# Four GNN layers on one core: the first layer's turns, gathers and normalizations in another order, the fourth layer's source rows made in the third, and loads issued a chunk sooner

## The reference

```python
x = _layernorm(x + attention(x, edge_attr))              # "layer 0"
x = _layernorm(x + relu(([x, mean of x[src]] @ W1 + b1) @ W2 + b2))   # "layer 1"
x = _layernorm(x + segment_sum((x @ weight)[src, rel], dst))          # "layer 2", 8 relations
x = _layernorm(x + update_by_node_type([relu(x), 3 typed message sums]))  # "layer 3"
```

## Time and profile before

| what | value |
|---|---|
| median of 3 runs | 1717.78 us (1715.58 to 1718.99) |
| profiled execution | 1722.77 us, span 1721.0 us |
| mean granted TensorE clock | 0.923 |
| busy: PE, DVE, ACT, POOL | 1390.8, 1410.1, 1120.2, 1230.3 us |
| layer 0 with its gathers | to 657 us |
| layer 1 | 667 to 957 us |
| layer 2 | 1009 to 1328 us |
| layer 3 | from 1343 us |

### The profile page before, as it was taken

How to read it: one execution, slowest core, us unless ns; L and a number is a source line. 1 busy time by engine, 2 the same in 40 slices (tenths; PEclk the granted TensorE clock), 3 DMA queues, 4 the chain that set the end, 5 groups by cost and what they waited for, 6 DMA issues and landing times.

```text
span 1721.0 us, 22842 instructions
## 1 busy us (share of the span) xinstructions
PE 1390.8 (81%) x6078; PEld 902.0 (52%) x6078; DVE 1410.1 (82%) x3005; ACT 1120.2 (65%) x2769; POOL 1230.3 (71%) x910
## 2 busy tenths in 40 slices
PE   4687777777777755787878589999998699999995
PEld 2454444544445434666666355555555355555552
DVE  4688888888888874998889679999998578877774
ACT  1567877778777783999999836666665344334442
POOL 7877777777788877778888387776330668888874
PEclk9678999999999987989999889999999899999998
DMA  7334444444434343677777535555543434333320
GB/s 169 85 68 101 112 98 98 105 104 112 99 98 108 82 130 73 187 201 192 197 196 194 161 87 144 150 141 137 148 119 94 99 94 101 99 94 93 98 74 22
DMA packets 165796, 205.06 MB, mean 119 GB/s; under 512 B 66825, under 2 KB 97920, under 8 KB 165668
## 3 DMA queue, kind: packets, MB, share of 16 engines
q1 hardware_dynamic: 108068, 179.45, 38.8%
q0 software_dynamic: 57600, 24.15, 8.0%
HBM read 147.12 MB, written 70.80 MB: 127 GB/s over the span
## 4 chain that ended last, share of the span: by engine, by line
PE 48%; DVE 16%; ACT 12%; issue 12%; POOL 9%; DMA 2%; SPq 1%; POOLq 0%; DVEq 0%; ACTq 0%
PE po L1323 22%; PE pt L1312 6%; POOL slot_all L528 6%; DVE masked L937 5%; DVE bst L732 4%; ACT x L1039 3%; PE pb L1329 2%; PE pb L1561 2%; PE po L1318 2%; PE po L1383 2%; PE pc L1431 2%; ACT so L1039 2%; PE pc L1312 2%; ACT do L1039 2%; ACT res L1039 1%
## 5 line engine op out<-in xcount | busy, mean ns | idle before, releaser
L528 POOL DMA_INDIRECT xs<-target_rows,slot_all x236 | 316.9, 1343 | 160.9 <-issue 68.8
L1039 ACT ACTIVATE x<-y,nmr,rst 125x128 f32<-125x128 f32 x800 | 322.3, 480 | 43.2 <-DVE nmr L757 43.2
L1323 PE MATMUL po<-wnt,rt 128*125 128x384 f32 x800 | 290.1, 508 | 0.0
L1312 PE MATMUL pt<-ident,x 125*128 125x125 f32 x800 | 134.6, 295 | 111.2 <-issue 82.3
L1323 PEld LDWEIGHTS po<-wnt,rt 128*125 128x125 f32 x800 | 158.3, 201 | 92.3 <-issue 14.4
L1323 PE MATMUL po<-wnt,run 128*125 128x384 f32 x600 | 201.5, 486 | 0.0
L535 POOL DMA_INDIRECT out_rows<-do,last_all x100 | 146.6, 1466 | 60.7 <-issue 40.0
L528 POOL DMA_INDIRECT xs<-in_x,src_all x100 | 133.8, 1338 | 53.7 <-issue 53.7
L1312 PEld LDWEIGHTS pt<-ident,x 125*128 125x128 f32 x800 | 100.1, 154 | 136.9 <-issue 100.9
L1039 ACT ACTIVATE do<-yd,nmr,rst 125x128 f32<-125x128 f32 x400 | 163.5, 482 | 6.2 <-DVE nmr L757 6.2
L1039 ACT ACTIVATE res<-sel,nmr,rst 125x128 f32<-125x128 f32 x400 | 163.5, 482 | 3.8 <-DVE nmr L757 2.6
(11 more groups left out here) (186 smaller groups left out, 3024.5 us busy)
## 6 DMA issues: line engine op xcount, KB each, us to landing
xin<-in_x SPq DMA_DIRECT2D x100, 224.0 KB
out_rows<-res SPq DMA_DIRECT2D x100, 224.0 KB
same<-same_d SPq DMA_DIRECT2D x75, 250.0 KB, 4.1
source_rows<-so SPq DMA_DIRECT2D x75, 224.0 KB
target_rows<-do SPq DMA_DIRECT2D x75, 224.0 KB
xs<-source_rows SPq DMA_DIRECT2D x59, 224.0 KB
rel<-in_etype SPq DMA_DIRECT2D x50, 250.0 KB, 4.8
xd<-target_rows SPq DMA_DIRECT2D x46, 224.0 KB
```

What stands on the lines that cost most here:

```text
L528: return nc.gpsimd.indirect_dma_start(out=to, out_offset=None, in_=table, in_offset=bass.IndirectOffsetOnAxis(ap=index, axis=0), bounds_ch ...
L1039: last = A(to[:, j, :], y[:, j, :], ACT.Identity, scale=rst[s][:, k:k + 1], bias=nmr[s][:, k:k + 1])
L1312: last = nc.tensor.transpose(tile_of(to, j), rows_[:, j, :], ident[0:R, 0:R])
L1323: last = mm(po[0:R, j * 512:j * 512 + NT * D], left(j), wnt[:, k, :, :].rearrange("k t d -> k (t d)"), start=start, stop=stop, skip_group_ ...
```

## The change

**In layer 0** the gathers of a chunk are split: the four of the sources wait only for what reads xs, then five marks instead of six, then the four of the targets. PE turns the sources of chunk c+2 ahead of the products of dense chunk 2c, and ACT takes its normalizations and evacuations in another order. SOONER goes from 19 to 13, so 52 instead of 76 slot gathers stand ahead of layer 1; the other 48 are issued within layer 1.

**In layers 1 and 2** the second normalization `so3` leaves layer 1. DVE makes instead one factor per row (factors1, two small operations per chunk, into again_all), and in layer 2 ACT makes the same rows as xs times that factor (source_rows2, four activations per chunk). SP stores them in layer 2.

**On SP** the first loads of layers 1, 2 and 3 stand ahead of the last stores of the layer before; the sums of layer 3 go to other buffers (aux and rel3).

The core of the diff:

```diff
-        MARKS = 6
+        MARKS = 5
         MARKED = -(-T * EC // MARKS)
-        SOONER = 19
...
+        SOONER = 13
+
...
                 sp.wait_ge(q["nS"], c + 1)
                 for part in PARTS:
                     sp.dma_start(rows(s_rows[1])[c][part, :], flat(so[b])[part, :]).then_inc(q["stS"][b], 16)
-                for part in PARTS:
-                    sp.dma_start(rows(s_rows[2])[c][part, :], flat(so3[b])[part, :]).then_inc(q["stS"][b], 16)
...
-            store_sources0(EC - 1)
...
+            rows1(2)
+            targets1(1)
+            store_sources0(EC - 1)
             store_targets0(EC - 2)
-            rows1(2)
             store_targets0(EC - 1)
-            targets1(1)
...
             def sources2(c):
                 k, q, o = c % 3, ph[2], ph[1]
                 sp.wait_ge(q["tS"], at(c - 2))
-                sp.wait_ge(o["stS"][c % 2], counted(c, 2 * ROWS))
+                sp.wait_ge(q["nS"], at(c - 2))
+                sp.wait_ge(o["stS"][c % 2], counted(c, ROWS))
...
+            def store_sources2(c):
+                b, q = c % 2, ph[2]
+                sp.wait_ge(q["nS"], c + 1)
+                for part in PARTS:
+                    sp.dma_start(rows(s_rows[2])[c][part, :], flat(so3[b])[part, :]).then_inc(q["stS"][b], 16)
...
+            for c in range(EC):
...
+                if c == EC - 1:
+                    sources2(0)
+                    relations2(0)
+                    sources2(1)
+                    relations2(1)
+                    sums2(0)
+                    targets2(0)
+                    sums2(1)
+                    sources2(2)
+                if c >= 1:
+                    store_sources1(c - 1)
+                    store_targets1(c - 1)
+                    store_dense(d - 7)
             store_targets1(EC - 1)
...
             stored(1)
+            store_sources2(0)
             sources2(3)
+            store_sources2(1)
...
+                sp.wait_ge(q["vA"], at((c - 1) * NT))
+                if c < 2:
+                    sp.wait_ge(ph[1]["vA"], EC)
+                sp.dma_start(aux[b][:, :], to_all(same_d, c)).then_inc(q["sm"][b], 16)
+                sp.dma_start(rel3[b][:, :], to_all(etype3, c)).then_inc(q["sm"][b], 16)
+
...
+                if c == EC - 1:
+                    sources3(0)
+                    targets3(0)
+                    sums3(0)
+                    sources3(1)
+                    sums3(1)
+                    sources3(2)
                 if c >= 1:
                     store2(c - 1)
+                if there(c + 2):
+                    store_sources2(c + 2)
                 store_dense(d - 7)
...
-            def rows0(c):
+            def sources0(c):
                 k, q = c % 3, ph[0]
                 for j in range(T):
-                    gather(xs[k][:, j, :], x, src_all[:, c, j:j + 1], N - 1).then_inc(q["g"][k], 16)
-                    gather(xd0[k][:, j, :], x, dst_all[:, c, j:j + 1], N - 1).then_inc(q["g"][k], 16)
+                    gather(xs[k][:, j, :], x, src_all[:, c, j:j + 1], N - 1).then_inc(q["gs"][k], 16)
+
+            def targets0(c):
+                k, q = c % 3, ph[0]
+                for j in range(T):
+                    gather(xd0[k][:, j, :], x, dst_all[:, c, j:j + 1], N - 1).then_inc(q["gd"][k], 16)
...
             for c in range(EC):
                 q = ph[0]
+                if there(c + 3):
+                    pool.wait_ge(q["yb"], c + 1)
+                    pool.wait_ge(q["tS"], c + 1)
+                    sources0(c + 3)
...
                     marks0(MARKS * c, MARKS * (c + 1))
...
                     slots1(MARKS * (c - MARKED), MARKS * (c - MARKED + 1), s_slot[0])
                 if there(c + 3):
-                    pool.wait_ge(q["yb"], c + 1)
                     pool.wait_ge(q["tD"], c + 1)
                     pool.wait_ge(q["nF"], c + 1)
-                    rows0(c + 3)
...
+                late = SOONER + 2 * (c // 3) + c % 3
+                if c % 3 < 2 and there(late):
+                    k, n = slot_ring(late)
+                    pool.wait_ge(s_slot[k], 16 * T * (n - 1))
+                    slots1(late * T, (late + 1) * T, s_slot[k])
+                elif c > EC // 2:
+                    types2(typed, typed + 2)
+                    typed += 2
+            types2(typed, typed + 2 * T)
+            typed += 2 * T
...
+            def factors1(c, s, third, first):
+
+                of = lambda a, g: a[s][:, g * T:(g + 1) * T]
+                step(V.scalar_tensor_tensor(out=of(tmp, 0), in0=of(ve, first), scalar=1.0 / D, in1=of(rst, first), op0=ALU.mult, op1=ALU.mult))
+                V.tensor_tensor(again_all[:, c, :], of(tmp, 0), of(rst, third), ALU.mult).then_inc(ph[1]["vF"], 1)
+
...
                 rows_of(2 * c, s, (4, 0))
+                if there(c + 1):
+                    results_of(2 * c, s, 2)
                 sums0(c)
-                if c < EC - 1:
-                    evacuate_dense(2 * c)
...
+                    evacuate_rt(2 * c)
+                    differences0(c + 1)
+                    evacuate_xt(2 * c)
                     weights0(c + 1)
+                if there(c + 2):
+                    evacuate_sources(c + 2, 0, 0)
                 rows_of(2 * c + 1, s, (5, 1))
                 source_rows0(c, s)
                 if c >= 1:
                     target_rows0(c - 1, s, 7)
-                if c == EC - 1:
+                if there(c + 1):
+                    evacuate_rt(2 * c + 1)
+                    results_of(2 * c + 1, s, 3)
+                    evacuate_xt(2 * c + 1)
+                else:
...
-                act.wait_ge(q["stS"][b], (c // 2) * 2 * ROWS)
-                normalize(so[b], ys[b], k % 2, 4)
-                normalize(so3[b], ys[b], k % 2, 1).then_inc(q["nS"], 1)
+                act.wait_ge(q["stS"][b], (c // 2) * ROWS)
+                normalize(so[b], ys[b], k % 2, 4).then_inc(q["nS"], 1)
...
+            def source_rows2(c):
+                b, q = c % 2, ph[2]
+                act.wait_ge(q["stS"][b], (c // 2) * ROWS)
+                for j in range(T):
+                    last = A(so3[b][:, j, :], xs2[c % 3][:, j, :], ACT.Identity, scale=again_all[:, c, j:j + 1], bias=none[:, 0:1])
+                last.then_inc(q["nS"], 1)
...
             evacuate_sources(0, 2, 7)
+            act.wait_ge(ph[1]["vF"], EC)
+            source_rows2(0)
             act.wait_ge(ph[2]["vM"], REL - 1)
             evacuate_sources(1, 2, 7)
+            source_rows2(1)
...
                 evacuate_xt(d - 1)
+                if there(c + 2):
+                    source_rows2(c + 2)
                 act.wait_ge(q["stD"][b], (c // 2) * ROWS)
                 normalize(do[b], yd[b], k % 2, 3).then_inc(q["nD"], 1)
...
                     turn_xt(2 * c)
-                    dense_products(2 * c)
-                    turn_rt(2 * c + 1)
                     if there(c + 2):
                         score_features(c + 2)
                         turn_sources0(c + 2)
+                    dense_products(2 * c)
+                    if there(c + 2):
                         pe.wait_ge(ph[0]["eS"], c + 3)
+                    turn_rt(2 * c + 1)
+                    if there(c + 2):
+                        score_sources(c + 2)
                     turn_xt(2 * c + 1)
                     if there(c + 2):
-                        score_sources(c + 2)
                         turn_targets0(c + 2)
                         score_targets(c + 2)
```

More of the change, by code:

```diff
@@ L134, in gnn_kernel @@
         aux = two(sb, "aux", [D, C])
-        rel = two(sb, "rel", [D, C], I32)
+        rel, rel3 = two(sb, "rel", [D, C], I32), two(sb, "rel3_", [D, C], I32)
         run, run2 = sb("run", [D, 3, C + 1]), sb("run2", [D, 3, C + 1])
@@ L182, in gnn_kernel @@
                **{k: [sem(f"layer{n}_{k}_{i}") for i in range(ring)] for k, ring in RINGS[n].items()}} for n in range(4)]
-        s_slot = [sem(f"layer1_slots_{i}") for i in range(EC - SOONER + 1)]
+        s_slot = [sem(f"layer1_slots_{i}") for i in range(1 + 3)]
         s_types = sem("s_types")
@@ L376, in _ @@
             stored(0)
-            for c in range(EC):
-                d = block_of(1, c)
-                load_dense(d + 3)
-                if there(c + 3):
-                    rows1(c + 3)
-                if there(c + 2):
-                    targets1(c + 2)
-                    sums1(c + 2)
-                if c >= 1:
-                    store_sources1(c - 1)
-                    store_targets1(c - 1)
-                    store_dense(d - 7)
             def sources2(c):
@@ L561, in _ @@
             pool.wait_ge(s_idx, 80)
-            for j in range(T):
-                gather(xs[0][:, j, :], x, src_all[:, 0, j:j + 1], N - 1).then_inc(s_first, 16)
-            for j in range(T):
-                gather(xd0[0][:, j, :], x, dst_all[:, 0, j:j + 1], N - 1).then_inc(ph[0]["g"][0], 16)
-            rows0(1)
-            rows0(2)
+            for c in range(3):
+                sources0(c)
```

(4 more changed lines are left out.)

132 lines of the change are left out of this document (57 added, 75 removed), and 2 rows, old and new, of the table RINGS.

## The result

The changed kernel takes 1842.01 us, median of 4 runs (1837.04 to 1843.65), against 1718.38 us before (4 runs): ratio 1.0716, 95% interval 1.069 to 1.0743. Predicted were 1818 us, between 1755 and 1868. The profiled execution has a span of 1841.9 us, 120.9 above that of the earlier trace rows.

A forecast was written before the change was run, and what follows sets the result against it. POOL bounds the stretch up to layer 1, DVE and ACT layer 1, DVE layer 2. 1722.8 - 61 - 7 - 3 + 176 - 5 = 1822.8, less 5.0 for the profiled execution, gives 1818 us, range 1755 to 1868.

The forecast's parts named there:

- term 4: Layer 2: SP's wait to store so3 delays rel, stretching chunks from 13.08 to 21.2 us, +176.
- term 1: Up to layer 1: 24 slot gathers fewer on POOL bring layer 1's first gather to 596, -61.
- bound of -40: POOL up to layer 1: the gain if POOL keeps all its waits of 25 us, -40.
- bound of -65: POOL up to layer 1: the gain if POOL has no waits, -65.
- terms 2 and 3: Layer 1, fewer ACT activations and DVE waits, -7; into layer 2, a shorter DVE wait for ACT's seed, -3.
- term 5: Into layer 3: loads now stand before the last store of `do`, so POOL waits less, -5 (0 to -7).
- B's sign: Layer 1's first gather after 615 us, the profile sign named for B.
- A: Layer 2: the wait in SP's queue does not bind, chunks stay at 13.08 us; 1644 us, chance 0.12.
- B: Layer 0 keeps 23.9 us per chunk, POOL gains 13 us instead of 61; 1866 us, chance 0.08.
- signs of being right: Layer 2: scans 19 to 22 us apart, DVE waiting 6; layer 1's first gather about 596; layer 0 chunks 21.5.

The follow-up runs named there:

- so3_first: The changed kernel with ACT making so3 at the head of its iteration in layer 2, SP's order as in the change: 1659.48 us.
- sp_order: The changed kernel with SP storing so3 one chunk later in layer 2 and loading xs behind the two stores: 1662.37 us.
- store_later: The changed kernel with only SP's store of so3 one chunk later in layer 2: 1777.96 us.
- slots_19: so3_first with SOONER back at 19, so 76 instead of 52 slot gathers stand ahead of layer 1: 1698.47 us.
- not_filled0: clock_kept0 without its two needless products per chunk, the moved products kept in their new places: 1636.72 us.
- clock_kept0: so3_first with layer 0's edge features' product moved into PE's first gap and made three times, the sources' product into the second: 1634.32 us.
- norm_kept1: so3_first with the four activations into so3 also kept in layer 1, their output unread: 1673.06 us.
- old_order0: so3_first with layer 0's order on PE and ACT as before the change, POOL as in the change: 1687.19 us.

## Why the prediction was right, point by point

**The store of so3 (term 4).** Predicted +176, measured +180.7, by the mechanism that was named: SP leaves its wait late in the next iteration, rel is late, DVE waits for it in front of the masks. so3_first and sp_order show it from both sides, and each gives back some 180 us. Three things were incomplete. The wait in the load of xs is a second link at the same place (store_later), and the prediction, which spoke of the store, did not weigh it. The link that holds st was named a place off: not DVE's masks, which are done by S+4.18, but PE's products and its turn behind them, and it is there that the half clock acts. And the parts of the sum were a little off: without the half clock the mean period is 19.6 us, not 18.8 (413/22), for in the chunks shown rel takes 5.2 to 5.5 us from issue to use instead of 4.8; and the clock's part is 1.6, not 2.2. That these two errors cancel, and +176 comes so close, is luck; the mechanism is not.

**POOL up to layer 1 (term 1), the step that was mis-sized.** Predicted -61, measured -41.9. It lies at the bound of -40 that kept all of POOL's waits. 24 instructions fewer are worth 39 us (slots_19), as worked out. The rest hung on ACT's 20.7 to 20.9 and DVE's 21.3 us per chunk; layer 0 ran at 23.0, so POOL, which needs 21.5, kept waiting. The term has no cost for PE's clock. The new order lines PE's waits up ahead of one group of products, and the clock of the layer falls from 0.93 to 0.87. With the two products moved into the gaps the predicted 21.3 are there (not_filled0, clock_kept0). So of the reordering's possible 2.7 us per chunk the change got 0.9; of the 1.7 that not_filled0 adds, 0.9 is shown to be the clock's. Two sizes were wrong besides. The bound of -65 without any wait is not the furthest, as clock_kept0 has its first gather at 583.60, 73.6 us sooner than the kernel before, so an instruction can cost less than 1.655. And 24, not 48, slot gathers move into layer 1: with SOONER at 19, the other 24 were there already.

**Layer 1 and the way into layer 2 (terms 2 and 3).** Predicted -10, measured -15.4; norm_kept1 puts 13.6 on the normalization alone. What makes the other 2 us, the earlier loads or something else, was not tried.

**Into layer 3 (term 5).** Predicted -5, measured -2.6. The last store of `do` is no longer behind loads, and POOL's first gather stands 25.4 us behind the last but one scan (1433.27 to 1458.71) instead of 32.9 (1309.81 to 1342.71); of these 7.5 us 4.9 are given back later, and where was not pursued.

**The rivals.** A's time, 1644 us, is what the change would have been worth without the stall: so3_first has 1659, and the 15 us between them are less than the 25 that clock_kept0 gives back in layer 0. B's sign, a first gather after 615 us, did come, by a hair (615.31), but its price did not: the pace moved by 0.9 of the possible 2.7 us, and the gather came 42 us sooner, not 13. B's own case is old_order0, with 23.9 us per chunk, where the gather is 20.7 us sooner. The two gains of layer 0 do not add up, for 38.5 us later (slots_19) and 24.6 later (old_order0) are together more than the 45.3 by which so3_first is ahead of the kernel before.

**The range.** By its own bounds the upper end of the sum is 1722.8 - 40 + 189 - 5 = 1867 us with the small terms at nothing, not 1850; the stated range, up to 1868, holds it all the same. Of the signs of being right the scans 19 to 22 us apart, rel as releaser, SP's wait for so3 and the clock of 0.83 came; DVE's wait was 8.3 us each time (173.3 in 21) instead of 6, and the first gather at 596 and the 21.5 us of layer 0 did not come.

## What to carry to other kernels

When a store is put into an in-order DMA queue, ask of its wait not how long it is, but whether what it waits for depends, through other engines, on something that stands behind it in the same queue: then it is no delay to be hidden but a ring, and every chunk pays its whole length. Such a ring is cut wherever it is cheapest, in the queue's order or in the producer's. And when work on PE is reordered, look where its waits come to stand next to each other, since the products behind them may run slower than the row that one costs them by: here 4.08 us instead of 2.74.

## What the runs showed of the hardware that was not expected

In layer 0 of so3_first, with PE busy for 82% of the time, the granted clock was 0.87 with idle times of 2.06, 1.44 and 0.68 us ahead of one group of products. It was 0.98 in not_filled0, where two products of 1 us each stand between them, although PE was idle in sum for longer there (72 of 358.5 us, against 63). So between these two kernels the clock did not go by the sum of the idle time but by where it lay. The waits of one chunk do not settle it alone either: in not_filled0 the products behind idle times of 1.28, 0.59 and 0.68 us took 2.74 us in one chunk (442.48), and 3.79 behind 1.29, 0.60 and 0.68 in the next (465.63). In layer 2 eleven products per chunk that do nothing took 37 us off the kernel.
